# Selective-scan and expert layers on one core: one pipeline by batch for the input of each scan

## The reference

```
x = x + layernorm(SSM0(layernorm(x)))     # selective scan, rank 64
x = x + layernorm(FFN0(layernorm(x)))     # sign-weight linear layer
x = x + layernorm(SSM1(layernorm(x)))     # selective scan, rank 128
x = x + layernorm(MoE(layernorm(x)))      # 16 experts, top 2, shared expert

SSM(x):  p  = x @ W_in                     # rank columns, then B (16), then C (16)
         dt = softplus(p[:, :rank] @ W_dt + b_dt)
         A  = -exp(A_log)                  # 256 x 16
         h[t] = exp(dt[t] * A) * h[t-1] + dt[t] * B[t] * x[t]
         y[t] = sum_n h[t] * C[t] + D * x[t]
```

## Time and profile before

| | |
|---|---|
| median of 3 runs | 792.56 us (791.62 to 793.7) |
| the profiled execution's own time | 792.4 us |
| its span in the trace | 790.5 us |
| busy: PE, DVE, ACT, POOL | 653.1 (83%), 574.4 (73%), 542.5 (69%), 453.2 (57%) us |
| input of scan 0 (start to the first L510) | 0 to 70.3 us |
| scan 0 (L510) | 70.3 to 237.6 us |
| end of scan 0 to the first L510 of scan 1 | 237.6 to 356.2 us |
| chain that ended last, by engine | PE 74%, DVE 13%, ACT 7%, POOL 3% |

### The profile page before, as it was taken

How to read it: one execution, slowest core, us unless ns; L and a number is a source line. 1 busy time by engine, 2 the same in 40 slices (tenths; PEclk the granted TensorE clock), 3 DMA queues, 4 the chain that set the end, 5 groups by cost and what they waited for, 6 DMA issues and landing times.

```text
span 790.5 us, 10083 instructions
## 1 busy us (share of the span) xinstructions
PE 653.1 (83%) x2907; PEld 417.3 (53%) x2909; DVE 574.4 (73%) x1137; ACT 542.5 (69%) x1213; POOL 453.2 (57%) x396
## 2 busy tenths in 40 slices
PE   3936999999994438648999999984989999999960
PEld 2325555555552324234555555543867777777640
DVE  6365999999997585649999999979583134444358
ACT  2769999999986775959999999956323322222225
POOL 0034999999994131048999999955047423333400
PEclk9956999999997577968999999995599999999986
DMA  6031444444430000012535444417012323333163
GB/s 165 6 67 36 133 140 133 140 133 142 131 115 1 0 1 3 18 58 94 149 118 160 134 134 149 131 46 231 1 54 94 105 96 107 106 105 103 64 219 107
DMA packets 57567, 77.65 MB, mean 98 GB/s; under 512 B 8113, under 2 KB 38481, under 8 KB 57521
## 3 DMA queue, kind: packets, MB, share of 16 engines
q1 hardware_dynamic: 53728, 66.75, 28.0%
q0 software_dynamic: 3792, 10.36, 3.7%
HBM read 58.21 MB, written 18.87 MB: 98 GB/s over the span
## 4 chain that ended last, share of the span: by engine, by line
PE 74%; DVE 13%; ACT 7%; POOL 3%; DMA 2%; issue 1%; SPq 0%; ACTq 0%; POOLq 0%; DVEq 0%
PE bank L1060 28%; PE bank L1050 14%; PE bank L1097 11%; DVE st L342 4%; PE bank L1105 3%; PE bank L1106 3%; PE bank L948 2%; PE bank L951 2%; POOL arena L896 2%; PE bank L961 2%; PE bank L934 2%; PE bank L970 2%; DVE tok_a L381 1%; ACT rings L793 1%; PE bank L1167 1%; DVE rings L686 1%
## 5 line engine op out<-in xcount | busy, mean ns | idle before, releaser
L881 POOL TENSOR_TENSOR arena<-arena,rings 128x512 f32<-128x512 f32 x256 | 321.6, 1283 | 31.3 <-DVE arena L510 26.9
L510 DVE TENSOR_TENSOR_SCAN arena<-rings,bank 128x512 f32<-128x512 f32 x256 | 296.2, 1200 | 15.9 <-PE bank L1050 7.1
L1060 PE MATMUL bank<-arena,ident 128*128 128x512 f32 x512 | 263.7, 601 | 0.0
L1050 PEld LDWEIGHTS bank<-ident,rings 128*128 128x128 f32 x1024 | 131.3, 145 | 143.8 <-issue 124.6
L793 ACT ACTIVATE rings<-tok_a,b_tok 128x256 f32<-128x256 f32 x448 | 191.0, 495 | 0.4 <-ACT tok_a L753 0.4
L803 ACT ACTIVATE rings<-arena,a_sb 128x512 f32<-128x512 f32 x256 | 169.1, 709 | 0.0
L1050 PE MATMUL bank<-ident,rings 128*128 128x128 f32 x1024 | 158.4, 280 | 11.3 <-ACT rings L793 10.9
L918 POOL DMA_INDIRECT y_tok<-rings,dest x47 | 44.9, 955 | 82.9 <-DVE rings L659 82.6
L1060 PEld LDWEIGHTS bank<-arena,ident 128*128 128x128 f32 x512 | 79.3, 193 | 5.7 <-issue 4.8
L857 ACT ACTIVATE silu<-bank 128x176 f32<-128x176 f32 x47 | 14.9, 317 | 85.5 <-PE bank L1097 85.5
L896 POOL TENSOR_TENSOR arena<-arena,feat_a 128x512 f32<-128x512 f32 x8 | 18.7, 2357 | 90.1 <-DVE arena L402 90.1
(11 more groups left out here) (160 smaller groups left out, 852.8 us busy)
## 6 DMA issues: line engine op xcount, KB each, us to landing
rings<-c_rows SPq DMA_DIRECT2D x128, 256.0 KB, 3.3
w_sb<-w SPq DMA_DIRECT2D x18, 352.0 KB, 4.1
x_sorted<-zeros SPq DMA_DIRECT2D x47, 128.0 KB, 3.2
rings<-x_sorted SPq DMA_DIRECT2D x47, 128.0 KB, 2.0
arena<-w SPq DMA_DIRECT2D x2, 2048.0 KB, 12.3
residual<-x SPq DMA_DIRECT2D x4, 512.0 KB, 6.1
tok_a<-y_tok SPq DMA_DIRECT2D x4, 512.0 KB, 7.3
w_sb<-y_tok SPq DMA_DIRECT2D x4, 512.0 KB, 8.1
```

What stands on the lines that cost most here:

```text
L510: dve.tensor_tensor_scan(state[:, u % STATE_RING, :], abar[:, u % ABAR_RING, :], bank[u % B_RING][:, :], 0.0, ALU.mult, ALU.add).then_inc( ...
L881: pool.tensor_tensor(s, s, crep[:, k % CREP_RING, :], ALU.mult).then_inc(hc_ready, 1)
L1050: ins = pe.transpose(bank[u % B_RING][:, j * P:(j + 1) * P], v_ring[:, s % V_RING, j, h * P:(h + 1) * P], ident[:, :])
L1060: pe.matmul(ysum_of[b % 2][h][:, :], ident[:, :], state[:, u % STATE_RING, :], start=n == 0, stop=n == N - 1).then_inc(state_free, 1)
```

## The change

The two lists become one of ten stages: x_stat, x_norm, turn, proj, pre, b_cols, err, log, dt, u_turn. The new stage b_cols does something only for q = 3: on PE the transposes of `b_columns(l)`, on DVE the copy of `b_columns(l)` and, for l = 0, `ssm_weights(0)`; on ACT, for l = 0, the two Exp of A_log. ACT loads one table that holds exponential and logarithm ahead of the first Relu of stage pre for q = 0 in each layer.

```diff
-        into_ssm = ["x_stat", "x_norm", "turn", "proj", "pre", "err"]
-        softplus = ["log", "dt", "u_turn"]
+        into_ssm = ["x_stat", "x_norm", "turn", "proj", "pre", "b_cols", "err", "log", "dt", "u_turn"]
...
+                elif name == "b_cols":
+                    if q == Q - 1:
+                        b_columns(l)
+                        if l == 0:
+                            ssm_weights(0)
                 elif name == "err":
...
             dve.tensor_copy(ident_bf[:, :], ident[:, :]).then_inc(fsign_in, 1)
-            ssm_weights(0)
-            b_columns(0)
-            for name, q in in_turn(softplus):
-                stage(name, q, 0)
             scan(0)
...
             for name, q in in_turn(out_of_ssm + ffn + into_ssm):
-                stage(name, q, 1)
-            b_columns(1)
-            for name, q in in_turn(softplus):
                 stage(name, q, 1)
             scan(1)
...
+                elif name == "b_cols":
+                    if l == 0 and q == Q - 1:
+                        for i in range(2):
+                            act.wait_ge(ld_ssm[i], 80)
+                            act.activation(a_sb[i][:, :, :], a_sb[i][:, :, :], ACT.Exp).then_inc(a_exp_ready, 1)
                 elif name == "pre":
+                    if q == 0:
+                        act.preload_act_table_set("natural_log_exp_and_others")
...
             for name, q in in_turn(into_ssm):
                 stage(name, q, 0)
-            for l in range(2):
-                act.wait_ge(ld_ssm[l], 80)
-                act.activation(a_sb[l][:, :, :], a_sb[l][:, :, :], ACT.Exp).then_inc(a_exp_ready, 1)
-            for name, q in in_turn(softplus):
-                stage(name, q, 0)
             scan(0)
...
+                elif name == "b_cols":
+                    if q == Q - 1:
+                        b_columns(l)
                 elif name == "gate":
...
             for name, q in in_turn(into_ssm):
                 stage(name, q, 0)
-            b_columns(0)
-            for name, q in in_turn(softplus):
-                stage(name, q, 0)
             scan(0)
             for name, q in in_turn(out_of_ssm + ffn + into_ssm):
-                stage(name, q, 1)
-            b_columns(1)
-            for name, q in in_turn(softplus):
                 stage(name, q, 1)
             scan(1)
```

## The result

The changed kernel takes 795.36 us, the median of 5 runs (793.87 to 796.45), against 792.56 (791.62 to 793.7): ratio 1.0029, 95% interval 1.0017 to 1.0042. It is slower by 1.3 to 3.3 us. I had forecast 797.2, 4.7 us slower. The sign is right and the time lies in the range. The size is too large: 1.7 times against the 2.8 us between the medians, twice against the 2.3 us that the ratio gives. The profiled execution has a span of 792.1 us; it is the shortest of the five, 1.5 us above the profiled one of before.

The account below looks back on a forecast made before the run. The prediction took DVE's string before each scan, holding POOL's first product, as the bound. Scan 0 +4.8 - 1.28 = +3.5 and scan 1 +2.5 - 1.28 = +1.2 gave 792.4 + 4.7, rounded 797.2 us; range 793.6 to 799.6.

Parts of the forecast that it names:

- DVE's wait in b_cols: Ahead of each scan, DVE idles for PE's transposes, about 6.6 and 4.6 us, with err 2 queued behind.
- ACT's and PE's unchanged order: After stage pre of batch 3, both keep their old order, but for ACT's two small Exp.
- The load ahead of each scan: ACT's table load right before the scan's first exponential goes, bringing 1.28 us for each scan.
- the load ahead of the logarithms: ACT's table load at 47.01, beside DVE's string; removing it brings nothing.
- The scans' length: ACT's list in the scan isn't changed, so the length stays at 167.3 us.
- DVE's own durations: On DVE before each scan: err of a batch takes 3.27 us, dt of a batch 1.81.
- with DVE in one string, POOL's first product ends at 61.54: Before scan 0, POOL is held until DVE's string ends, ending at 61.54 instead of 56.73; chance 0.45, 797.2 us.
- several turns: Rival before the scans: POOL and DVE take turns for each product, 790.5 to 795.3 us; chance 0.11.
- PE's clock: In a rival, PE's turns before the scans: 1.96 us each at the low clock; which clock was left open.
- one turn at the pause of `settle()`: Rival: POOL's first product gets in at DVE's pause behind err 3, 795.1 to 799.4 us; chance 0.28.
- +4.8 up to dt 3: Before scan 0, POOL's first product and all that follows, dt 3 included, come 4.8 us later.
- 2.66 us with a drain: Rival on ACT's table loads: each of two brings about 2.7 us, sum about 794.4; chance 0.04.

Follow-up runs that it names:

- e3: Changed kernel with DVE's copy of B and sign change of A moved from b_cols to right before the scan: ratio 0.9959 to the kernel before.
- e2: Kernel before with the joint exponential and logarithm table alone, all orders as before: ratio 0.9966, 2.7 us faster.
- e1: Kernel before, unchanged, profiled once more on another chip: ratio 0.9999.
- e10: Kernel before with a DVE pause ahead of dt 0, then one extra DVE instruction in layer 0, four in layer 1: ratio 1.0051.

## Why the prediction was right, and where it was not

**Right.** DVE's wait in b_cols, with err 2, err 3 and all dt behind it: 7.36 + 1.30 us and 4.81 us against the forecast 6.6 and 4.6 for the first part, and e3 shows that the kernel is faster than before once it is gone. ACT's and PE's unchanged order. The load ahead of each scan is worth its time and the load ahead of the logarithms nothing (e2). The scans' length. DVE's own durations: err 2 started at 47.90 (48.16 forecast), dt 0 at 51.10 (51.53). Of the 0.3 to 0.4 us, 0.2 is that ACT ends the Exp of batch 3 earlier, and I had counted nothing there. Whether the load's new place does that isn't shown: two executions of the kernel before lie 0.4 us apart at POOL's first product (51.47, and 51.90 in e1).

**Wrong: the step "with DVE in one string, POOL's first product ends at 61.54".** It ended at 54.11. I had read from two products of 5.26 us that POOL stands still as long as DVE runs, and took it for the rule for any such string. The two rows were one case, a long unbroken string, seen in two layers. What the changed kernel does is what I had as "several turns": a turn for each product, three in all that hold DVE, 1.2 us of DVE's time each by my reckoning and 1.07 as measured. I had given it 0.11 and worked its end with 1.2 to 795.3. That this is the median to 0.1 us is in part luck: that sum puts all three holds ahead of dt 3, where only two lie, has none of PE's clock below, and comes to +2.9 at the start of scan 1, where +2.0 was measured. The rival of one turn at the pause of `settle()` was half right: there is a pause, but POOL got in at borders without one too, at 52.9 and 59.0.

**By terms.** Layer 0: in place of +4.8 up to dt 3, dt 3 starts at 61.86 instead of 60.06, +1.8, because log 3 is ready early. To that come the hold in dt 3, 1.07 us (2.28 on the chain where it was 1.30), which gives +2.8 at POOL's last product, and 0.7 us from there to the last copy. The latter I had only in a rival: PE's clock. The window of the last turn, before and after:

```profile
63.10:64.50 1.40, 1.20 (x8) 0.84 (x8) 0.00 (x0) 1.22 (x3) 0.00 (x0) 1.00 0.00 0
```

```profile
66.00:68.00 2.00, 1.94 (x8) 1.57 (x8) 0.02 (x1) 0.60 (x1) 0.00 (x0) 0.50 0.00 0
```

Before, the four turns came close behind each other, with PE standing at most 0.4 us between them, and the granted clock was back at 2.4 GHz for the last one (1.00). After, POOL's products release them one by one, the last three 2.9 us apart; PE stands for 4.1 us ahead of the second turn and for 0.9 ahead of the third and fourth, and the last one is at 1.2 GHz (0.50). Sum +3.6. Layer 1 has the same parts, -0.6 up to dt 3, +1.0 by the hold in it, +0.8 by the clock (1.00 before, 0.50 after): +1.2 instead of +2.5. The load I had at 1.28, measured 1.42, twice. Together 3.6 - 1.4 + 1.2 - 1.4 = +2.0 at the start of scan 1, against +4.7. The 2.7 us that I forecast too much are the product that didn't stand still, less the clock, and 0.3 of the loads.

**Two rules against the rows.** The page "SBUF — State Buffer" of the Trainium skill, section SBUF: two separate sides, says that whichever starts first of a GpSimd instruction and a DVE instruction that needs the shared ports has them for the whole instruction, and the other is blocked. The holds of 1.07 us agree. The row of 5.26 us had made me give more weight to the string than to turns. What the page doesn't say is that case, in which POOL was passed over at six borders. On the price of a load, "ScalarE: Activation LUTs" of the Trainium skill, section What ACT_TABLE_LOAD costs, has 2.66 us with a drain; e2 and the changed kernel show 1.42 on the chain, so that figure would have been wrong here. The page doesn't say on which side of the load the drain lies; before, the load at 68.13 began 0.02 us after the activation ahead of it, and the next followed it by 0.02, so the trace has none on either.

## What to carry to other kernels

A stage that needs all batches, put into a pipeline by batch, makes an in-order engine wait at its place in the list: put it where its input is long there, here behind dt 3. Before one relies on a row in which one engine waits for another, one should ask what around it made it so; two layers of the same code are one observation. And a small elementwise product can be cheapest on the engine that it would otherwise hold up, as here: 0.60 us of DVE's own against 1.07 us held or 4 us waited.

## What the hardware did that I had not expected

A POOL tensor_tensor of 128x512 from SBUF takes 1.27 us beside an idle DVE. Beside a DVE that runs SBUF-only instructions it took 1.64 us and held DVE's next instruction for 1.07 us, when DVE had stood at most 4 instructions (1.7 us) before POOL's request, or right after it. A gap of 0.03 to 0.1 us was enough for that, where DVE's instructions otherwise overlap by 0.08, and so, by the rows, was a hold by POOL. It took 5.25 us and held nothing when DVE's string ahead of it was 7 to 11 instructions and no gap followed. The outcome repeated in every execution that was profiled: two of the kernel before, on two chips, e2 with the same string and e10 in layer 1 (5.25 us each), and all products beside a running DVE in the other kernels (1.63 to 1.65 us).
